# The first layer's projections and scores in three bf16 parts instead of two f32r parts

## What is computed

```
x  = x + L0_attn(layernorm(x))
x  = x + L0_ffn(layernorm(x))
x  = x + L1_attn(layernorm(x))          # linear attention, gated
x  = x + L1_ffn(layernorm(x))

def L0_attn(x):
    xq, xk, xv = x @ Wq, x @ Wk, x @ Wv  # 32 heads, 8 heads, 8 heads of 16
    xq, xk = rotary(xq), rotary(xk)      # x0 cos - x1 sin, x0 sin + x1 cos
    scores = xq . xk / sqrt(16), causal
    return softmax(scores) . xv @ Wo
```

## Time and profile before

| what | us |
|---|---|
| median of three runs | 3348.85 |
| the runs | 3347.05 to 3355.23 |
| the profiled execution's own device time | 3353.35 |
| its span, first to last instruction | 3351.6 |
| busy: TensorE, weight loads | 3151.9 (94%), 2543.6 (76%) |
| busy: VectorE, ScalarE, GpSimd | 1281.3 (38%), 1299.6 (39%), 989.6 (30%) |
| mean granted TensorE clock, share of 2.4 GHz | 0.949 |

### The profile page before, as it was taken

The page is one execution under the profiler, slowest core; times in us unless marked ns, Lnnn a source line. Parts: engine busy times, 40 slices in busy tenths (PEclk is TensorE's granted clock), DMA queues, the critical chain, the costliest instruction groups (busy, mean ns, idle before and its releaser), DMA issues. The chain is left out here.

```text
span 3351.6 us, 53397 instructions
## 1 busy us (share of the span) xinstructions
PE 3151.9 (94%) x19288; PEld 2543.6 (76%) x19288; DVE 1281.3 (38%) x2211; ACT 1299.6 (39%) x2281; POOL 989.6 (30%) x844
## 2 busy tenths in 40 slices
PE   6699999988699999999999998999999999999978
PEld 5444444446588888888888887888888888888866
DVE  5376666634632223322223324222332223322258
ACT  2145565552133334333343333334333334333321
POOL 3422222210423333323333232333333333323321
PEclk9769998878899999999999998999999999999989
DMA  4512222200111111111111111111111111111101
GB/s 148 179 34 31 44 30 36 39 2 3 48 35 34 44 44 34 37 48 41 47 34 34 50 34 35 35 46 41 34 44 40 44 44 34 34 50 37 49 21 51
DMA packets 99497, 146.88 MB, mean 44 GB/s; under 512 B 29584, under 2 KB 43280, under 8 KB 97876
## 3 DMA queue, kind: packets, MB, share of 16 engines
q1 hardware_dynamic: 86552, 126.30, 12.2%
q0 software_dynamic: 12864, 19.48, 3.7%
HBM read 125.27 MB, written 19.92 MB: 43 GB/s over the span
## 5 line engine op out<-in xcount | busy, mean ns | idle before, releaser
L1425 PE MATMUL bank<-l_xT_hi,l_w_T 128*128 128x512 f32 x3072 | 788.8, 399 | 0.0
L1425 PEld LDWEIGHTS bank<-l_xT_hi,l_w_T 128*128 128x128 f32 x3072 | 556.0, 188 | 103.9
L1355 DVE TENSOR_TENSOR l_sc<-bank,l_mask 128x512 f32<-128x512 f32 x128 | 88.5, 692 | 955.6 <-PE bank L1481 942.4
L688 ACT ACTIVATE att_exp<-bank 128x512 f32<-128x512 f32 x576 | 321.3, 598 | 256.7 <-PE bank L785 241.5
L1425 PE MATMUL bank<-l_xT_lo,l_w_T 128*128 128x512 f32 x1536 | 412.6, 390 | 0.0
L728 DVE TENSOR_REDUCE att_max<-bank 128x2 f32<-128x1024 f32 (+2 forms) x320 | 342.2, 1113 | 174.5 <-PE bank L769 99.5
L1222 POOL TENSOR_TENSOR l_w_T<-l_w_raw,l_w_T 128x512 fp32r<-128x512 f32 x198 | 255.5, 1291 | 513.2 <-ACT l_w_T L1267 513.2
L1425 PEld LDWEIGHTS bank<-l_xT_lo,l_w_T 128*128 128x128 f32 x1536 | 288.4, 188 | 63.8
L1425 PE MATMUL bank<-l_o_T,l_y_hi 128*128 128x512 f32 x1024 | 323.4, 392 | 7.2 <-DVE l_y_lo L1327 7.2
L1425 PE MATMUL bank<-l_v_T,l_xT_hi 128*128 128x256 f32 x2048 | 295.2, 285 | 3.4 <-DVE l_xT_lo L986 3.4
L785 PE MATMUL bank<-att_QT,att_KT 50*128 50x512 f32 (+3 forms) x768 | 266.4, 439 | 33.8 <-ACT att_exp L688 31.0
(11 more groups left out here) (216 smaller groups left out, 4614.1 us busy)
## 6 DMA issues: line engine op xcount, KB each, us to landing
l_w_raw<-in_L_attn_qkv_w SPq DMA_DIRECT2D x198, 256.0 KB, 2.8
l_w_raw<-in_L_attn_gate_w SPq DMA_DIRECT2D x66, 256.0 KB, 2.7
l_o_raw<-in_L_attn_out_w SPq DMA_DIRECT2D x33, 512.0 KB, 3.7
query_parts<-att_exp SPq DMA_DIRECT2D x48, 256.0 KB
att_QT<-query_parts POOLq DMA_DIRECT2D x32, 384.0 KB, 7.9
att_KT<-key_parts POOLq DMA_DIRECT2D x32, 192.0 KB, 6.2
X<-in_L_attn_x SPq DMA_DIRECT2D x4, 1024.0 KB, 11.2
l_mask<-in_decay SPq DMA_DIRECT2D x32, 128.0 KB, 2.1
```

The source lines that it names most:

```text
L688: nc.scalar.activation(E[:, U % RING, j, :], ps_t[i % 2], ACT.Exp, scale=SCALE).then_inc(e_ready, 1)
L1355: dve.tensor_tensor(sc[:, half(s)].rearrange("p (c n) -> p c n", n=P), ps_a[n % NA][:, :].rearrange("p (c n) -> p c n", n=P), mask[:, h, : ...
L1425: mm = pe.matmul(out, lhs, rhs, start=(n == 0), stop=(n == len(pairs) - 1))
```

## The change

- The rotated queries and keys are split into three bf16 parts (high, middle, low) in place of high and low f32r parts. ScalarE copies the high and the middle part, GpSimd subtracts the high one in place (`rest`), VectorE subtracts the middle one (`low`). Each item is stored three times, as before, now at half the bytes. The rows are ordered by channels of one head.
- A group's queries and keys stand in SBUF once, in 96 rows (six products of parts) and three rows for the maximum in three parts; scores for the maxima and for the exponentials are bf16 matmuls over 96 and 99 rows, one head at a time. The mask is one matmul of 128 rows. There are 22 slots a group instead of 20.
- A group is loaded with six DMAs instead of four; these and the maxima's DMA (one for two) are issued by SP. The first three groups are loaded after the stores of the third block, ahead of those of the fourth.
- The values are the first weight tile of a block; their copy has its own place in a third products buffer, and they are transposed after the block's third tile.
- ScalarE normalises x with a bias and a scale (VectorE makes the bias with one small operation a block). VectorE takes the statistics of a block further ahead, spread between products.
- Rows of -1 are set by VectorE; the two halved constants are replaced by an identity and one mask.

```diff
-QKV_TILES = ("qA0", "qB0", "qA1", "qB1", "kAB", "kBA", "v")
+QKV_TILES = ("v", "qA0", "qB0", "qA1", "qB1", "kAB", "kBA")
-PARTS = 2
+PARTS = 3
-STACK = 3 * HEAD_DIM
-ROWS = STACK + PARTS
+STACK = 6 * HEAD_DIM
+ROWS = STACK + MAX_PARTS
...
             @block.sync
-                    sp.wait_ge(staged_hi, item + 1)
-                    sp.wait_ge(staged_lo, item + 1)
-                    for part, at in PLACES[m == ITEMS - 1]:
+                    for part, ready in enumerate((staged_h, staged_m, staged_l)):
+                        sp.wait_ge(ready, item + 1)
...
+                        sp.dma_start(to, stage(item, part)).then_inc(stored[n % 2], 16)
+                    if item == ITEMS * (BLOCKS // BATCH + 1) - 1:
+                        for one in stored[1:]:
+                            sp.wait_ge(one, 16 * STORES)
+                        sp.wait_ge(stored[0], 16 * STORES * 2)
+                        for g in range(KEPT):
+                            load_group(sp, g)
...
             @block.gpsimd
+                        for item in items(n, i):
+                            pool.wait_ge(staged_h, item + 1)
+                            nc.gpsimd.tensor_tensor(rotated_tile(item), rotated_tile(item), stage(item, 0), ALU.subtract
+                                                    ).then_inc(rest, 1)
...
             @block.scalar
+                def middle(item):
+                    act.wait_ge(rest, item + 1)
+                    nc.scalar.copy(stage(item, 1), rotated_tile(item)).then_inc(staged_m, 1)
+                def normalize(t):
+                    act.wait_ge(offset_done, t // BLOCK_TILES + 1)
+                    if t >= 2:
+                        act.wait_ge(transposed, t - 1)
+                    nc.scalar.activation(xn[:, t % 2, :], X[:, t, :], ACT.Identity, bias=offset[:, t:t + 1],
+                                         scale=rstd[:, t:t + 1]).then_inc(normed, 1)
...
                 for n in range(BLOCKS):
+                    if more:
+                        normalize(x)
+                        normalize(x + 1)
+                    if n:
+                        high(first - 1)
+                    keep_v(n)
+                    if n:
+                        middle(first - 1)
+                    if more:
+                        high_x(x)
+                        normalize(x + 2)
+                        high_x(x + 1)
+                        normalize(x + 3)
+                    lay_v(n)
+                    high(first)
+                    high(first + 1)
+                    if more:
+                        high_x(x + 2)
+                    middle(first)
+                    middle(first + 1)
+                    if more:
+                        high_x(x + 3)
+                    high(first + 2)
+                    high(first + 3)
+                    middle(first + 2)
+                    middle(first + 3)
...
             @block.vector
+                def low(item):
+                    dve.wait_ge(staged_m, item + 1)
+                    dve.tensor_tensor(stage(item, 2), rotated_tile(item), stage(item, 1), ALU.subtract
+                                      ).then_inc(staged_l, 1)
...
                 for n in range(BLOCKS):
+                    for k in range(1, NT):
+                        if n and k == 3:
+                            low(ITEMS * n - 1)
+                        multiply(n, k)
+                        if k <= BLOCK_TILES:
+                            if n + 1 < BLOCKS:
+                                low_x(x + k - 1)
+                            if n + 2 < BLOCKS:
+                                count(x + BLOCK_TILES + k - 1)
+                        if k == 4:
+                            low(ITEMS * n)
+                            low(ITEMS * n + 1)
                     if n + 2 < BLOCKS:
                         scale(n + 2)
+                    low(ITEMS * n + 2)
+                    low(ITEMS * n + 3)
...
             @block.tensor
-                        if k == 0 and n:
-                            turn_v(n - 1)
+                        if k == 2:
+                            turn_v(n)
...
+def load_heads(sp, g, QT, KT, Q_dram, K_dram, q_in, k_in):
+    slot, at = g % KEPT, 0
+    for part, count in ((0, 3), (1, 2), (2, 1)):
+        rows = slice(HEAD_DIM * at, HEAD_DIM * (at + count))
+        key = K_dram[g, HEAD_DIM * part:HEAD_DIM * (part + 1), :]
+        sp.dma_start(KT[rows, slot, :], key.unsqueeze(0).broadcast_to([count, HEAD_DIM, SEQ])).then_inc(k_in[slot], 16)
+        sp.dma_start(QT[rows, slot, :, :], Q_dram[REP * g:REP * (g + 1), 0:HEAD_DIM * count, :].rearrange("h r n -> r h n")
+                     ).then_inc(q_in[slot], 16)
+        at += count
...
+        SLOTS = [(0, (0, 1, 2, 3), P), (1, (0, 1, 2, 3), 2 * P), (2, (0, 1), 512), (2, (2, 3), 512),
+                 (3, (0, 1), 512), (3, (2, 3), 512)] + [(q, (j,), 1024) for q in range(4, 8) for j in range(REP)]
...
             @block.sync
+                for g in range(GROUPS):
+                    sp.wait_ge(s_read, IN_S[("turn_max", g)] + 1)
+                    sp.dma_start(QT[STACK:ROWS, g % KEPT, :, :].rearrange("m h (q n) -> m h q n", n=P),
+                                 mx_T[:, g % 2, :]).then_inc(max_in[g % KEPT], 16)
+                    if g >= 1 and g + KEPT - 1 < GROUPS:
+                        sp.wait_ge(t_ready, REP * NU * g)
+                        load_group(sp, g + KEPT - 1)
...
                 def scores_for_max(slot, g, k):
+                    for h, j in enumerate(heads):
+                        for a in range(0, (q + 1) * P, 512):
+                            b = min(a + 512, (q + 1) * P)
+                            to, diagonal = h * step, b == (q + 1) * P
+                            mm = pe.matmul(flat[:, to + a:to + b], QT[0:STACK, g % KEPT, j, q * P:(q + 1) * P],
+                                           KT[0:STACK, g % KEPT, a:b], start=True, stop=not diagonal)
+                            if diagonal:
+                                mm = pe.matmul(flat[:, to + b - P:to + b], ident_b[:, :], mask_s[:, :],
+                                               start=False, stop=True)
```

420 lines of the change are left out of this document (169 added, 251 removed).

## The result

| kernel | median, us | runs | ratio to before, 95% interval |
|---|---|---|---|
| before | 3350.19 | 3347.05 to 3355.23 | |
| after | 3267.95 | 3265.73 to 3272.29 | 0.9758 [0.9743, 0.9773] |

The account below looks back on a forecast made before the run. It took the projection as slowed by waits around TensorE and SP's stores at its end, and attention as bound by no engine alone. Projection -18 us and attention 0, from 3348.85, gave 3331 us, range 3300 to 3368.

Parts of the forecast that it names:

- nearer the bytes: End of projection: SP's last fifteen stores cost 9 to 17 us, by bytes or by pieces; attention's start taken as 140.
- VectorE's move: Projection: VectorE gives up four normalisations and takes five low parts, +0.85 us, about 18 a block, below TensorE's 21.5.
- Rival 3: Projection gains nothing at its end, from SP's stores or the chain of parts; attention starts at 150 to 155; 3343; chance 0.18.
- -1.2 + 1.4 + 0.3 - 0.5: Attention, per group: score latency, lost pairing, VectorE's extra maxima and clock, taken together as 0 for attention.
- (a): Attention's score loop: bf16 weights load faster, perhaps 0.1 us per two scores; -1.8 us a group at most, -1.2 taken.
- no engine is the bound alone: Attention before the change: VectorE 21.5, ScalarE 20.2 and TensorE 37.7 us a group, TensorE's matmuls overlapping and busy mostly with latency.
- (b): Attention's maxima: scores lose their pairing of two heads, up to +4.1 us of TensorE a group; +1.4 taken.
- (c): Attention: VectorE has 22 maxima a group for 20 over the same elements; +0.3 us a group.
- a third of the 4.1: Attention: the share of the extra TensorE time from unpaired maxima that was put on the path, +1.4 us a group.
- My sum of TensorE's columns: Attention: by columns TensorE has some 25 of 34 us a group, values 7.7 to 8 of them, and 29 after.
- The clock, -0.5: Attention: a group loses about 1.5 us to 1.2 GHz stretches; more columns streamed should mean fewer, -0.5 us a group.
- rival 2: Attention: denser stream holds 2.4 GHz, clock above 0.97, -1.6 us a group more; 3305; chance 0.17.

Follow-up runs that it names:

- a_norm: The changed kernel with the normalisation of x put back on VectorE, all else kept; 3271.1 us.
- a_f32r_scores: The changed kernel with only the operands of the scores for the exponentials read as f32r (values meaningless), the maxima's kept in bf16; 3300.9 us.
- a_f32r_max: The changed kernel with only the operands of the maxima's scores read as f32r (values meaningless); 3295.0 us.
- b_bf16: The kernel before with the operands of both score passes read as bf16 (upper halves of the f32r numbers), heads still in pairs; 3308.6 us.
- b_bf16_double: The kernel before with bf16 score operands, still in pairs, and each pair of the maxima's matmuls issued twice; 3307.8 us.
- b_keep: The kernel before with ScalarE's copy of the values put ahead of the copy of the block's last rotated item; 3332.8 us.
- a_f32r: The changed kernel with the operands of both score passes read as f32r (scores meaningless), in full tiles; 3323.5 us.
- a_load2: The changed kernel with a four-column matmul of the same weights ahead of each score and maxima matmul, so each weight loads twice; 3293.8 us.
- a_both: The changed kernel with the second and third groups loaded when attention begins and the rows of -1 written early by GpSimd; 3252.76 us.

## Why the prediction was wrong

**The projection, right, in part by luck.** Attention began at 139.1 for a forecast of 140 (136 to 144). Blocks came 22.3, 23.5 and 20.5 us apart for 22.5; the wait of TensorE for the values' copy is gone; the granted clock is 1.00. On SP the loads took 14.5 us for 13, and ended at 120.3, 2.7 us earlier than I had them. The fifteen stores took 11.1 us. My 140 leaves 13.3 for them (140 - 3.7 - 123), which is the middle of 9 to 17 and not "nearer the bytes"; a query store took 9.13 / 12 = 0.76, between the 0.58 by bytes and the 1.16 by pieces. The change of stage took 4.3 for 3.7. One step was missing from the sum: the rows of -1. From the stage's first instruction on SP to the first matmul it is 3.4 us, 2.6 of them that memset. So -2.7 - 2.2 + 0.6 + 3.4 = -0.9: a missing step made up for loads and stores that came early. I had priced VectorE's move at 0.85 us a block and held that it has room; a_norm shows what hung on the move: with 17 to 19 us of VectorE in each of the first two blocks they take 22.3 and 23.5 us, with 22 they take 25.5 and 24.1, and attention starts 6 us later. Whether its load or the place of the four normalisations in its queue does that was not separated. Rival 3, which did not happen, took 1.6 us for a store; no row has that, gives 1.16 and 1.95.

**Attention, wrong, by the terms of its sum.** I had -1.2 + 1.4 + 0.3 - 0.5, so 0 a group, and it was -3.9. That is beyond my own bound of -3.3, and by the sign that I had named, a group that changes by over 1.2 us, the prediction fails as a whole. Two terms failed: the type of the maxima's operands, which the sum has at nothing and which measured 1.45 us, and the clock, which it has at -0.5 and which is left with some -2.0.

(a) The latency of the scores, -1.2 with -1.8 as its bound. The size of one step was right: 0.10 us less from weights to exponential. That was luck in its ground, since the 0.29 and 0.50 us that I compared are four matmuls of 128 columns and one of 512, not weight loads; the loads' own rows in that trace, 97 ns in bf16 and 187 to 189 in f32r, would have carried it. But I charged the type to the scores alone. a_f32r_scores gives 1.55 us for them, inside the bound, and a_f32r_max another 1.45 for the maxima, for which the sum had nothing. The earlier trace rows showed the sign: ScalarE idle for 69.6 us of 175, of which 64.5 for the scores' banks (L785), and VectorE for 47.5, nearly all for the maxima's. I read from the same rows that "no engine is the bound alone" and took TensorE's time as latency to be hidden. An engine for which both the others wait, in one fixed order, sets the pace, and its instructions count: not always in full (1.4 of the 4.1 us of doubled pairs), but not at nothing either.

(b) The lost pairing, +1.4. b_bf16 to b_bf16_double, the same columns twice at the full clock, gave +1.4 in the groups that had it before (30.1 to 31.5), and b_bf16 to after +0.9 (30.1 to 31.0) in the same groups, with (c) in it. The place and the sign were right. The size was luck: no row stood behind "a third of the 4.1". My sum of TensorE's columns was wrong too. It has 7.7 to 8 us of values a group; in the trace of before four value matmuls of 512 columns, one a head, start together, and the next four 0.45 and 0.43 us later (343.30, 343.75, 344.18), so the nine units of a group take 3.9 us, and TensorE had some 21 of 34 us by columns, not 25.

(c) VectorE's two more maxima: not measured by themselves. Its maxima take 108.8 us in five groups for 107.5, +0.3 a group, as priced.

The clock, -0.5. Here I took the wrong base: 34.2 us was the mean of two ordinary groups, and I called what was above it the loss, 1.5 us, and gave back a third. After has none of it: its mean, 31.89, is that of its ordinary groups, 31.9, so this profile gave back all 1.5. Some 1.1 of it need no change of attention, as b_keep shows. And the two groups themselves stand at 0.95 in the earlier trace rows and at 1.00 in after. What that is worth by itself no run shows; in b_bf16 the ordinary group at 0.90 takes 34.7 us, and 32.9 in b_bf16_double at 1.00, although with more columns. With 0.99 over the fifteen groups this was rival 2's case, and it has its mark, "clock above 0.97". Rival 2's step, that the other 1.0 of the 1.5 us comes back, was right; it gave 3305 because it, too, had nothing for the maxima's type.

Put together from ordinary groups at 1.00: type -2.8 (a_f32r to after), tiles with (c) +0.9 (30.1 to 31.0), so -1.9 of the -3.9. The +0.9 is from the one ordinary length that both kernels have at 1.00. The other 2.0 are a remainder, which I put down to the clock: 1.5 by the slow groups, and 0.5 for the ordinary ones going from 0.95 to 1.00. That is a difference and not a measurement; by means it is -3.0 for the type in pairs (35.75 to 32.77) and -0.9 for the tiles (to 31.89), with the clock in both. The last group's -8.5 was not taken apart; b_bf16 has -3.0 of it.

**The page of the Trainium skill that spoke against the change** (TensorEngine Tiling (Array Packing), Overview and Tiling Modes: row tiles give up to twice the rate) is borne out in small: pairs are 0.9 to 1.4 us a group cheaper at the same clock (30.1 for 31.0 and 31.5). The rule that bears on the weight loads I had not weighed. The trace shows a weight load of 128 columns at 97 ns in bf16 and 187 to 193 in f32r. By the Trainium skill (TensorE: Matmul & The Clock Gate, Weight-path perf modes) the compiler switches on a faster way of loading when the number of weights is 128 and their type is not FP32, and it was measured at about twice the speed. The trace agrees with the ratio, 187 / 97 = 1.9. It does not show whether this way of loading is the cause. Nor do the loads explain the whole: a_load2, with each load made twice, brings back 1.15 of the 2.8 us.

**What stays open.** Why a matmul with f32r operands holds the order up by more than its load; how much of the gain in attention is the clock by itself, and why before and b_keep, alike there, differ by 16 us; which of the moves gives the second half of the projection's block; and why attention's first 36.8 us still pass at a clock of 0.50 (the stretch without a matmul ahead of it is 17.4 us long in before, 26.6 in after and 11.6 in a_both, and the first exponential comes 35.6, 36.8 and 37.4 us after the first matmul).

## What to carry to other kernels

When two engines both wait on a third, whose instructions go in one fixed order, take that third for the bound even if its busy time is made of latencies: give every instruction in its order a price, also those whose results are not urgent. A change of operand type reaches every matmul that reads the operand, so price it for each reader. And compare clocks before calling an ordinary group "full speed": pairs with bf16, the cheaper form, took 30.1 us at 1.00 and 34.7 at 0.90 in turn, where full tiles took 31.0 and 32.8 at 1.00. Before a small difference of means is put down to a change, look at a run that does not touch the stage: here such a run moved it by 16 us. At the end of a stage, read the queue that issues the stores: twelve of the eighteen early loads ahead of fifteen late stores cost 11 to 12 us here, and one small memset 3 to 4.

## What the runs showed of the hardware

- Weight loads of 128 columns of queries or keys: 96 to 98 ns in bf16, 187 to 193 in f32r, in tiles of 48 as of 96 rows. From the start of a score's weight load to its exponential 0.43 us in bf16, 0.53 in f32r. A matmul of four columns is recorded with 170 ns; the instructions by line of a_load2, in its groups from 301.8 to 460.4 us:

```profile
L805 PE MATMUL bank<-att_QT,att_KT 99*128 99x4 bf16 x232 | 38.6, 170 | 1.7 <-ACT att_exp L710 0.7
```

- The granted clock of the fifteen groups was 0.88 in before and 0.92 in b_keep, with the same matmuls in them (0.95 in the ordinary groups of both), 0.96 (1.00 in the ordinary ones) with the maxima's matmuls doubled, 0.92 with bf16 in pairs, 0.98 with these doubled, 0.99 in full tiles.
- A store of 128 KB in 128 pieces took 0.76 us of SP's queue when many were waiting, one of 256 KB 1.16; in a_both, where the stores follow the staging, it is 0.67 (8.05 / 12).
- A memset of three rows of 3072 bf16 takes VectorE 2.62 us, and TensorE waited for it.
